# Each engine's branch placed ahead of the last unit's tail, x added in PSUM, a shorter rounding, and key and query loads issued earlier on the DMA queue

## What is computed

```
x = x + attention(layernorm(x))        # 16 heads of 8, scores * exp(-1e-4 |i-j|)
y = layernorm(x) as bf16
q = fp8_e4m3(y / s_in);  k = fp8_e4m3(kernel / s_k)
x = x + (bf16(q @ k * s_in * s_k) + bias)
```

## Time and profile before

| | |
|---|---|
| median of 3 runs | 519.67 us (519.64 to 519.73) |
| the profiled execution's own time | 519.81 us |
| its span, first to last instruction | 518.0 us |
| PE busy | 478.4 us (92%) |
| ACT busy | 484.7 us (94%) |
| DVE busy | 270.4 us (52%) |
| last DVE write of the result ends | 513.7 us |

### The profile page before, as it was taken

The page is one execution under the profiler, slowest core; times in us unless marked ns, Lnnn a source line. Parts: engine busy times, 40 slices in busy tenths (PEclk is TensorE's granted clock), DMA queues, the critical chain, the costliest instruction groups (busy, mean ns, idle before and its releaser), DMA issues.

```text
span 518.0 us, 9463 instructions
## 1 busy us (share of the span) xinstructions
PE 478.4 (92%) x3452; PEld 112.4 (22%) x3452; DVE 270.4 (52%) x646; ACT 484.7 (94%) x535; POOL 218.7 (42%) x285
## 2 busy tenths in 40 slices
PE   8899999999999999899999999899999989899961
PEld 3312221132222212132122122123121212121220
DVE  6514553556545554445653654545645564455546
ACT  3789999999999999899999999899999999999951
POOL 0889409883810269692530239883100121002110
PEclk9999999999999999999999999999999999999995
DMA  6679989777444206747853123847835222300000
GB/s 180 196 245 219 328 188 234 285 238 224 126 108 114 76 13 198 234 103 241 257 117 90 46 66 127 246 130 249 251 88 127 66 65 68 88 21 2 1 22 24
DMA packets 57395, 73.79 MB, mean 142 GB/s; under 512 B 6976, under 2 KB 33024, under 8 KB 57344
## 3 DMA queue, kind: packets, MB, share of 16 engines
q1 hardware_dynamic: 56256, 72.72, 49.0%
q10 hardware_dynamic: 1088, 0.41, 0.3%
HBM read 35.40 MB, written 35.65 MB: 137 GB/s over the span
## 4 chain that ended last, share of the span: by engine, by line
PE 39%; ACT 33%; issue 11%; DVE 7%; POOL 4%; SPq 3%; DMA 3%; DVEq 0%; ACTq 0%; POOLq 0%
ACT probs L790 32%; PE ps L990 20%; PE ps L974 12%; DVE ps L1233 2%; PE ps L970 2%; PE ps L887 1%; PE ps L850 1%; PE ps L882 1%; DMA kp_dram<-parts 1%; POOL sq L614 1%; SPq L477 1%; DVE pv_out L1241 1%; POOL sq L626 1%; POOL parts L628 1%; PE ps L854 1%
## 5 line engine op out<-in xcount | busy, mean ns | idle before, releaser
L790 ACT ACTIVATE probs<-ps 128x1024 f32<-128x1024 f32 x512 | 473.6, 1101 | 8.9 <-DVE ps L1233 5.7
L990 PE MATMUL ps<-probs,V 128*9 128x512 f32 x2048 | 267.8, 595 | 1.0 <-ACT probs L790 0.6
L1233 DVE TENSOR_TENSOR ps<-ps,consts 128x256 f32<-128x256 f32 (+1 forms) x256 | 140.6, 563 | 160.9 <-PE ps L974 154.4
L974 PE MATMUL ps<-Qs,Ks 64*128 64x512 bf16 x992 | 172.2, 384 | 16.8 <-ACT probs L790 14.6
L974 PEld LDWEIGHTS ps<-Qs,Ks 64*128 64x128 bf16 x992 | 44.5, 93 | 286.9 <-ACT probs L790 275.2
L1241 DVE COPY pv_out<-ps 105x512 f32<-105x512 f32 x31 | 21.4, 691 | 60.0 <-PE ps L990 59.9
L592 POOL TENSOR_SCALAR rs<-mv 128x4 f32<-128x4 f32 (+1 forms) x10 | 2.3, 229 | 99.9 <-DVEq L1415 99.3
L990 PEld LDWEIGHTS ps<-probs,V 128*9 128x9 f32 x2048 | 30.5, 88 | 63.4 <-issue 53.9
L675 POOL TENSOR_TENSOR xs<-xs,magic 128x512 f32<-128x512 f32 x7 | 8.9, 1276 | 58.5 <-DVE magic L1294 58.5
L688 POOL TENSOR_TENSOR yb<-yb,bias_s 128x512 bf16<-128x512 bf16 x7 | 8.1, 1156 | 49.9 <-DVE yb L1366 49.5
L628 POOL TENSOR_TENSOR parts<-sq,parts 128x1024 bf16<-128x1024 f32 (+1 forms) x16 | 28.3, 1771 | 1.3
(11 more groups left out here) (148 smaller groups left out, 280.5 us busy)
## 6 DMA issues: line engine op xcount, KB each, us to landing
Qs<-qp_dram SPq DMA_DIRECT2D x58, 256.0 KB, 4.9
qp_dram<-parts SPq DMA_DIRECT2D x14, 768.0 KB, 6.1
Ks<-kp_dram SPq DMA_DIRECT2D x28, 256.0 KB, 3.9
kp_dram<-parts SPq DMA_DIRECT2D x12, 384.0 KB, 4.2
kp_dram<-parts SPq DMA_DIRECT2D x6, 768.0 KB, 5.0
Ks<-kp_dram SPq DMA_DIRECT2D x34, 128.0 KB, 2.9
qp_dram<-parts SPq DMA_DIRECT2D x7, 512.0 KB, 8.0
X<-L_attn_x SPq DMA_DIRECT2D x9, 256.0 KB, 2.9
```

Of the source, the lines that this page charges most:

```text
L790: nc.scalar.activation(probs[:, quad % RING, 2 * jp:2 * jp + 2, :].rearrange("p j n -> p (j n)"), ps_all[:, bank * CH:(bank + 2) * CH], AC ...
L974: last = nc.tensor.matmul(bank, Ks[half, g, jp, key_cols(v, kc)], Qs[half, g, jp, qh, v, :], start=True, stop=True)
L990: last = nc.tensor.matmul(pv[32 * j:32 * j + VW, :], V[:, unit // 2 * NB + kc, HG * j + g, :], probs[:, quad % RING, j, :], start=i == 0, ...
L1233: nc.vector.tensor_tensor(own, own, factors, ALU.mult).then_inc(fixed, 1)
```

## The change

1. **Branches.** Each engine loads the flag and branches before its last steps; these steps (`last_unit` on DVE with everything from the last `pv` copy on, `last_steps` on ACT and PE, `store_last` on SP) stand in both ways of the branch, so the Else now holds work.
2. **x in PSUM.** PE multiplies the unit matrix with `X1` into banks 4 and 5 before the last `weigh`, and the projection adds to it (`start=False`). The DVE adds L1476 go; statistics, normalised rows and the last adds read PSUM. For that, tokens of the last unit are laid out as `(p t)`, so that `pv` is copied with a stride of 4 elements in its four groups.
3. **Rounding.** Four DVE operations in place of six; ACT makes two more scaled copies (`wide`, `sq`) and takes over the scale of `y`. The pieces are 384 and 128 columns in place of two of 256.
4. **Loads.** `stage_second` moves to directly behind `gather`.

```diff
@@ SP
-                sp.dma_start(X1[...], x[rows(unit % UNITS), :].rearrange("(t p) d -> p t d", p=P))
+                order = "(p t) d -> p t d" if unit == LAST else "(t p) d -> p t d"
...
                     if unit < UNITS - 1:
                         gather(group)
+                    if qh == 0 and b > 0:
+                        stage_second(b, g)
...
-                    if qh == 0 and b > 0:
-                        stage_second(b, g)
...
             general = sp.value_load(flag[0:1, 0:1], min_val=0, max_val=1)
             with sp.If(general > 0):
+                store_last()
...
             with sp.Else():
-                sp.nop()
+                store_last()
@@ ACT
+            act.wait_ge(flag_ready, 1)
+            general = act.value_load(flag[0:1, 0:1], min_val=0, max_val=1)
             for half in range(2):
                 act.wait_ge(back_ps, half + 1)
                 nc.scalar.copy(OT[...], ps[:, 2 + half, 0:HALF])
+            def last_steps():
+                deviation(2, mv2, rs2)
+                for i in range(2):
+                    act.wait_ge(xn2_ready, i + 1)
+                    nc.scalar.activation(xs[:, cols], xn2[:, cols], ACT.Copy, scale=rscales[:, 0:1])
+                    act.wait_ge(xs_ready, i + 1)
+                    nc.scalar.activation(wide[:, cols], xs[:, cols], ACT.Copy, scale=2.0 ** -20)
+                    nc.scalar.activation(sq[:, 0, cols], xs[:, cols], ACT.Copy, scale=OVER_464)
+                for i in range(2):
+                    act.wait_ge(*xqT_ps_halves[i])
+                    nc.scalar.activation(xqT[:, piece_cols[i]], ps[:, 6 + i, :]..., ACT.Copy, scale=-2.0 ** 20)
+                    act.wait_ge(*y_ps_halves[i])
+                    nc.scalar.activation(yb[:, piece_cols[i]], ps[:, i, 0:n], ACT.Copy, scale=oscale[:, 0:1])
@@ PE
             weigh(QUADS - 2)
+            pe.wait_ge(x1_in[LAST % 2], 16 * (LAST // 2 + 1))
+            for half in range(2):
+                nc.tensor.matmul(ps[:, 4 + half, 0:HALF], eye[:, :], X1[:, LAST % 2, half_cols[half]],
+                                 start=True, stop=False)
             weigh(QUADS - 1)
@@ DVE
-                nc.vector.tensor_copy(pv_out[0:96 + VW, group % 2, :], pv[0:96 + VW, :])
+                if group >= LAST * G:
+                    nc.vector.tensor_copy(pv_out[...].rearrange("p (t n) -> p t n", t=4), pv_tiles)
...
-                step(nc.vector.tensor_tensor(own[:, half_cols[half]], ps[:, 4 + half, 0:HALF], own[:, half_cols[half]], ALU.add))
-                    step(nc.vector.bn_stats(stats2[:, t, :], own[:, t * D:(t + 1) * D]))
+                        step(nc.vector.bn_stats(stats2[:, t, :], sums[t]))        # sums: PSUM
...
+                    dve.wait_ge(xs_ready, i + 1)
+                    step(nc.vector.tensor_scalar(mh, xs, 0x7F800000, 0x00400000, ALU.bitwise_and, ALU.bitwise_or))
+                    dve.wait_ge(xm_ready, i + 1)
+                    step(nc.vector.scalar_tensor_tensor(out=xh, in0=mh, scalar=1.5 * 2.0 ** -6, in1=xh, op0=ALU.max, op1=ALU.add))
+                    step(nc.vector.scalar_tensor_tensor(out=xh, in0=mh, scalar=1.5 * 2.0 ** -6, in1=xh, op0=ALU.max, op1=ALU.subtract))
+                    dve.wait_ge(over_ready, i + 1)
+                    nc.vector.scalar_tensor_tensor(out=xn2[:, cols], in0=sq[:, 0, cols], scalar=0.0, in1=xh, op0=ALU.mult, op1=ALU.add)
```

More of the change, by code:

```diff
@@ L32 @@
 NAN_SCALE = 3.0e38 / (464.0 * 464.0)
+OVER_464 = 7.333670881280613e+35
 TABLE = 2 * S - P
@@ L312, in build @@
         xs_ready = sem("xs_ready")
+        xm_ready = sem("xm_ready")
+        over_ready = sem("over_ready")
+        ys_ready = sem("ys_ready")
         stored_half = sem("stored_half")
@@ L328, in build @@
         half_tiles = [slice(2 * h, 2 * h + 2) for h in range(2)]
+        piece_tiles = (range(0, 3), range(3, 4))
+        piece_cols = (slice(0, 3 * P), slice(3 * P, CH))
         o_tok = o_raw[:, LAST % 2, :].rearrange("p (t c) -> p t c", t=4)
+        pv_tiles = pv[0:96 + VW, :].rearrange("p (n t) -> p t n", t=4)
         rec_tok = rec[:, 0:4 * HG].rearrange("p (t j) -> p t j", t=4)
@@ L463, in load_x1 @@
                     sp.wait_ge(stored[unit % 2], 16 * (unit // 2))
+                order = "(p t) d -> p t d" if unit == LAST else "(t p) d -> p t d"
                 sp.dma_start(X1[:, unit % 2, :].rearrange("p (t d) -> p t d", d=D),
-                             x[rows(unit % UNITS), :].rearrange("(t p) d -> p t d", p=P)).then_inc(x1_in[unit % 2], 16)
+                             x[rows(unit % UNITS), :].rearrange(order, p=P)).then_inc(x1_in[unit % 2], 16)
             def store_result(unit):
@@ L545, in _, with store_last @@
                         load_x1(unit + 1)
[L546 to L551, removed]
+            def store_last():
+                for i in range(2):
+                    sp.wait_ge(*res_halves[i])
+                    sp.dma_start(out[rows(LAST), :].rearrange("(p t) d -> p (t d)", p=P)[:, piece_cols[i]],
+                                 X1[:, LAST % 2, piece_cols[i]]
+                                 ).then_inc((stored_half, stored[LAST % 2])[i], 16)
+                sp.wait_ge(kt_out, 16 * B)
+                sp.wait_ge(qt_out, 16 * B)
+                sp.wait_ge(stored_half, 16)
+                for i in range(2):
+                    sp.wait_ge(stored[i], 16 * B)
             sp.wait_ge(flag_ready, 1)
             general = sp.value_load(flag[0:1, 0:1], min_val=0, max_val=1)
[L555 to L559, removed]
             with sp.If(general > 0):
+                store_last()
                 sp.dma_start(g_table_s, decay_table[:, :]).then_inc(g_table, 16)
@@ L799, in _ @@
                 nc.scalar.copy(OT[:, LAST % 2, half_cols[half]], ps[:, 2 + half, 0:HALF]).then_inc(ot_halves[half][0], 1)
[L800 to L811, removed]
+            def last_steps():
+                deviation(2, mv2, rs2)
+                for i in range(2):
+                    act.wait_ge(xn2_ready, i + 1)
+                    cols = piece_cols[i]
+                    nc.scalar.activation(xs[:, cols], xn2[:, cols], ACT.Copy, scale=rscales[:, 0:1]).then_inc(xs_ready, 1)
+                    act.wait_ge(xs_ready, i + 1)
+                    nc.scalar.activation(wide[:, cols], xs[:, cols], ACT.Copy, scale=2.0 ** -20).then_inc(xm_ready, 1)
+                    nc.scalar.activation(sq[:, 0, cols], xs[:, cols], ACT.Copy, scale=OVER_464).then_inc(over_ready, 1)
+                for i in range(2):
+                    n = len(piece_tiles[i]) * P
+                    act.wait_ge(*xqT_ps_halves[i])
+                    nc.scalar.activation(xqT[:, piece_cols[i]], ps[:, 6 + i, :].bitcast(BF16)[:, 0:n], ACT.Copy,
+                                         scale=-2.0 ** 20).then_inc(xqT_halves[i][0], 1)
+                    if i == 0:
+                        act.wait_ge(res_ready, LAST)
+                    act.wait_ge(*y_ps_halves[i])
+                    nc.scalar.activation(yb[:, piece_cols[i]], ps[:, i, 0:n], ACT.Copy, scale=oscale[:, 0:1]).then_inc(ys_ready, 1)
             with act.If(general > 0):
+                last_steps()
                 for b in range(B):
@@ L821, in _ @@
             with act.Else():
-                act.nop()
+                last_steps()
         @block.tensor
@@ L941, in job @@
                     multiply(i, work)
+            pairs = (range(0, 2), range(2, 4))
             pe.wait_ge(eye_in, 16)
@@ L1035, in _ @@
             weigh(QUADS - 2)
+            pe.wait_ge(x1_in[LAST % 2], 16 * (LAST // 2 + 1))
+            for half in range(2):
+                nc.tensor.matmul(ps[:, 4 + half, 0:HALF], eye[:, :], X1[:, LAST % 2, half_cols[half]],
+                                 start=True, stop=False)
             weigh(QUADS - 1)
-            pairs = (range(0, 2), range(2, 4))
             for half in range(2):
@@ L1050, in _, with last_steps @@
                     last = nc.tensor.matmul(ps[:, 4 + half, t % 2 * P:t % 2 * P + P], OT[:, LAST % 2, t * P:(t + 1) * P],
-                                            wo_s[:, :], start=True, stop=True)
+                                            wo_s[:, :], start=False, stop=t % 2 == 1)
                 last.then_inc(proj_halves[half][0], 1)
[L1053 to L1066, removed]
+            def last_steps():
+                for i in range(2):
+                    pe.wait_ge(*xq_halves[i])
+                    if i == 1:
+                        pe.wait_ge(y_ready, LAST)
+                    for t in piece_tiles[i]:
+                        last = nc.tensor.transpose(ps[:, 6 + i, :].bitcast(BF16)[:, t % 3 * P:t % 3 * P + P],
+                                                   xn2[:, t * P:(t + 1) * P], eye16[:, :])
+                    last.then_inc(xqT_ps_halves[i][0], 1)
+                    pe.wait_ge(*xqT_halves[i])
+                    for t in piece_tiles[i]:
+                        last = nc.tensor.matmul(ps[:, i, t % 3 * P:t % 3 * P + P], xqT[:, t * P:(t + 1) * P], kq[:, :],
```

(22 more changed lines are left out.)

57 lines of the change are left out of this document (55 added, 2 removed).

## The result

The changed kernel takes 513.1 us (513.05 to 513.29, 4 runs) beside 519.7 for the kernel before in the same series: a ratio of 0.9874 (95% interval 0.9856 to 0.9891), 6.6 us faster. The prediction was 513.55, with a range of 512.7 to 515.5. The profiled execution took 513.14 us for a span of 511.3.

What follows compares the result with a forecast made beforehand. ACT, nearly always busy, bounds the loop apart from two gather waits; a chain through PE, DVE and ACT bounds the tail. Loop 3.42 plus 2.7 at the end (tail 1.32, branch 1.38) gave 513.55 us, range 512.7 to 515.5.

Steps and rivals of the forecast that it cites:

- Loads: In the loop: the last group's gather, 5.0 us earlier, ends two DVE waits of 1.71 us each: 3.42 gained.
- The join: Tail, before the last `weigh`: PE's two unit-matrix products make it start 0.2 to 0.5 us later, taken as +0.27.
- taking the two adds away: Tail, ahead of the normalised rows: two DVE adds go, each freeing 0.41 to 0.42 us; -0.81 in all.
- my reading of PSUM's cost: Tail: statistics, normalised rows and last adds reading PSUM charged nothing; the skill page's figure would add 0.45 us.
- Strided copy: Copies of `pv`: no penalty, 0 taken; other bound +0.4 us per half in the tail, +0.69 for three group copies.
- Rounding: Tail, from normalised rows to the last DVE write: 7.9 us in place of 8.68, -0.78.
- Branches: All engines' branches hidden ahead of their last steps; the uncovered branch at the span's end gives 1.38 us.
- landing 2.45 later: End of the span: the result's last store lands 2.45 us after the last DVE write, at 514.9.
- The loop that gives nothing: Rival: gather lands earlier, but ACT still stands at quad 7 for DVE's operations there; 517.0 us, chance 8%.
- the code fetch on ACT: Rival: ACT's branch takes 2.8 to 3.6 us and delays the root, +0.5 to +1.3 us; chance 14%.
- the slow strided copy: Rival: `pv` copies twice as long, +0.8 us in the tail, up to 3 x 0.69 in the unit; chance 11%.
- the second fetch: Rival: code behind the branch is cut by another fetch, every engine stands again in its tail; 522.7 us, chance 3%.

Runs made afterwards that it cites:

- branches-alone kernel: The kernel before with only each engine's branch moved ahead of its last steps, old instructions and old store kept: 517.9 us, ratio 0.9964.
- PE's late branch: The changed kernel with PE's flag load and branch alone put back behind its last product: 515.07 us, ratio 0.9903.
- kernel of equal pieces: The changed kernel with pieces of 256 and 256 columns in place of 384 and 128: 512.46 us, ratio 0.9855.

## Why the prediction was right

- **Loads.** Predicted -3.42, measured -3.34 within the change, and alone -3.2 against 519.7 or -3.5 against its own series' 519.99. The mechanism held. The estimate of the gather's last issue was 1.4 us too early: I kept the durations of its issues, though it now follows the store directly. A step of 59.17 stays against 59.11.
- **x in PSUM.** The join was priced at +0.27 and cost 0.38; taking the two adds away gave 0.93, not 0.81: 0.86 from the adds themselves, because the second half's statistics follow the first's without a gap, and 0.07 because DVE's first operation starts sooner. Here my reading of PSUM's cost failed in part. I charged nothing, from one row of an add. The tensor-scalar rows show 0.340 from SBUF and 0.404 from PSUM, while adds and statistics show no difference. It cost 0.2 in the rounding part, three rows in series. The Trainium skill (VectorE: DVE Perf Modes, the errata section) has a fixed 58 cycles from SBUF and 120 from PSUM at 0.96 GHz, from which I estimate 0.065 us: the tensor-scalar rows agree with it, the other two forms don't.
- **Strided copy.** No penalty in any of its five places, as L1315's slope said. Group copies take 0.690 to 0.692 without a stride and 0.690 to 0.691 with it, the two half copies 0.76 together in both kernels.
- **Rounding.** -0.78 predicted, -0.64 measured; without the 0.2 for PSUM it is -0.82. ACT's `wide` took 0.52 where I had 0.63, which was on the cautious side, and the way back was a little longer than I said.
- **Branches.** All are hidden, as forecast: the branches-alone kernel has its last write where it was. DVE's code was there in time, and PE's 3.60 us (from 499.06) end 2.6 us before its next product. The term was mis-sized all the same, -1.38 for -2.07, and outside its own bounds of -1.2 to -1.6. The step that failed is "landing 2.45 later": I took the store's landing as fixed, and it was 1.64. Of the 0.8 us, the branches-alone kernel shows 0.6 without any change to the store, and PE's late branch shows that a code fetch beside the store delays it. Of the rest, 0.1 goes with the new layout (128 KB land in 1.71 in the kernel of equal pieces, in 1.81 with the branches alone) and 0.07 with the smaller last piece (1.71 to 1.64).
- **Rivals.** The loop that gives nothing, the code fetch on ACT, the slow strided copy and the second fetch are all refuted by these rows. That the total came within 0.5 us owes something to misses of both signs: loads, join and rounding gave 0.33 less than forecast, the adds and the end 0.81 more.

What stays open is whether the fetch and the store share one DMA engine, as the 18 late packets suggest, and why the delay was 0.6 us in one kernel and 2 in another. The fetch's own packet was longer too: 2.0% of 16 engines' time over 5 us is 1.6 us with PE's branch late, and 2.4% over 2.8 us is 1.1 us in the kernel before. With PE's branch late the executions also scatter more (514.71 to 515.66), and 0.5 us of the slowest stand ahead of the last exp, so not all of that is the store.

## What to carry to other kernels

Look at the last instruction of each engine, not only at the last result: a branch over a long body cost 2.8 to 4.1 us here, and it costs nothing where the engine waits anyway. On a DMA queue in order, put what is ready ahead of what waits for another engine, and count the time of the short transfer behind it. In a tail cut in two pieces, compare what lies behind the last piece with what lies under it, and put extra products of PE into its waits one at a time.

## What the runs showed of the hardware that was new to me

- A code fetch delays data: a 128 KB store landed in 2.4 us with fetches beside it and 1.8 without, stores of 192 and 64 KB in 3.9 and 3.6 against 1.9 and 1.6. In the second case one sixteenth of the packets (18 of 288) came late, and the others no later than without a fetch.
- PE's branch took 3.4 to 3.7 us in the kernels that hide it; with stores beside it, 3.6 in the kernel before and 4.1 with PE's branch late. After DVE's, 2.8 us pass to its next instruction. ACT's and SP's, over shorter bodies, let the engine go on within 0.5 and 0.2 us.
- Reading PSUM instead of SBUF costs a tensor-scalar of 128 columns 0.064 us and an add of 256 columns nothing (0.423 and 0.424).
- An issue of a small DMA on SP takes 0.63 us. The first three directly behind the store of 2 MB of keys took 1.19, 1.38 and 0.95.
